# A reordered opening, and weights and the next rows held behind pair 0's gathers, in an attention, mixing and low-rank feed-forward kernel

## The reference

```python
# 1: attention over a block cache (window 128 + own tokens), 8 heads, 4 key heads of 32
q = rope(rms(x @ Wq.T) * (1 + qs), pos); k = rope(rms(x @ Wk.T) * (1 + ks), pos); v = x @ Wv.T
pos = lens[:, None] + arange(32)
k_blocks = k_blocks.at[table[b, pos // 16], :, pos % 16, :].set(k)   # and v_blocks with v
scores = q . k_all * SCALE, masked to pos - 128 < kpos <= pos
x = x + (softmax(scores) @ v_all) @ Wo.T
# 2, 3: a 32 x 32 matrix per sequence mixes its tokens; step 3 adds a bias
x = x + einsum(x, w1[cond]);  x = x + einsum(x, w2[subj]) + side[subj]
# 4: feed-forward, each linear with a low-rank part by the sequence's adapter
gate = x @ Wg + (x @ Ag[subj]) @ Bg[subj];  up = x @ Wu + (x @ Au[subj]) @ Bu[subj]
h = silu(gate) * up
x = x + h @ Wd + (h @ Ad[subj]) @ Bd[subj]
```

## Time and profile before

| | us |
|---|---|
| runs, median of 3 | 263.36 (260.64 to 263.76) |
| the profiled execution, own time | 262.86 |
| its span in the trace | 260.9 |
| PE busy, share of the span | 209.6, 80% |
| DVE busy | 140.6, 54% |
| ACT busy | 106.9, 41% |
| POOL busy | 82.8, 32% |
| mean granted clock of PE | 0.941 |

### The profile page before, as it was taken

The page is one execution under the profiler, slowest core; times in us unless marked ns, Lnnn a source line. Parts: engine busy times, 40 slices in busy tenths (PEclk is TensorE's granted clock), DMA queues, the critical chain, the costliest instruction groups (busy, mean ns, idle before and its releaser), DMA issues.

```text
span 260.9 us, 5090 instructions
## 1 busy us (share of the span) xinstructions
PE 209.6 (80%) x1993; PEld 190.3 (73%) x1993; DVE 140.6 (54%) x470; ACT 106.9 (41%) x290; POOL 82.8 (32%) x95
## 2 busy tenths in 40 slices
PE   2797969346858509994599979999988989989995
PEld 2785759245647408993598969988888989879995
DVE  1946877246675553396613763672375464135522
ACT  1615126587542551448102553381373345213310
POOL 3571037624467632007616036042421004000000
PEclk9979988968999956999689999999999999999999
DMA  6688979995863996753769202100400000010001
GB/s 192 153 178 142 168 185 237 433 189 86 133 186 97 256 170 81 105 82 92 149 122 178 71 3 71 32 0 23 123 0 3 0 1 3 3 40 3 0 0 43
DMA packets 64269, 26.28 MB, mean 101 GB/s; under 512 B 55941, under 2 KB 60933, under 8 KB 63653
## 3 DMA queue, kind: packets, MB, share of 16 engines
q1 hardware_dynamic: 60352, 15.07, 28.0%
q0 software_dynamic: 3104, 10.23, 16.3%
q10 hardware_dynamic: 788, 0.64, 0.8%
HBM read 18.87 MB, written 8.13 MB: 103 GB/s over the span
## 4 chain that ended last, share of the span: by engine, by line
PE 38%; issue 13%; DVE 12%; POOL 10%; SPq 10%; DMA 9%; ACT 7%; ACTq 0%; POOLq 0%; DVEq 0%
PE bank L1453 27%; SPq L612 5%; POOL far L685 4%; SPq L555 4%; ACT prob L806 3%; DVE prob L1097 3%; DMA near<-rows_of,place_i 3%; POOL prob L699 3%; DMA early<-in_kb,blk_i 3%; PE bank L1400 2%; PE bank L1439 2%; DMA k<-in_c 2%; DMA rows_of<-far_probs 2%; PE bank L1419 2%; DVE mask L1079 1%
## 5 line engine op out<-in xcount | busy, mean ns | idle before, releaser
L685 POOL DMA_INDIRECT far<-rows_of,place_i x32 | 32.3, 1008 | 63.3 <-issue 31.2
L806 ACT ACTIVATE prob<-prob,ntop,qscale 128x160 f32<-128x160 f32 x64 | 32.4, 508 | 15.7 <-DVE ntop L1103 15.7
L1453 PE MATMUL bank<-xf_high,gu_high 128*128 128x256 f32 x128 | 38.7, 303 | 0.0
L699 POOL TENSOR_TENSOR prob<-prob,rden 128x512 f32<-128x512 f32 x16 | 18.0, 1127 | 59.5 <-DVE rden L1109 59.5
L1453 PE MATMUL bank<-xf_high,gu_low 128*128 128x256 f32 x128 | 36.1, 282 | 0.0
L1453 PE MATMUL bank<-xf_low,gu_high 128*128 128x256 f32 x128 | 36.1, 282 | 0.0
L1133 DVE SCALAR_TENSOR_TENSOR gs<-th,bank 128x256 f32<-128x256 f32 x32 | 13.4, 420 | 28.5 <-ACT th L841 28.1
L1400 PE MATMUL bank<-k,prob 128*128 128x128 f32 x64 | 12.6, 329 | 17.9 <-POOL prob L699 17.9
L1453 PEld LDWEIGHTS bank<-xf_high,gu_high 128*128 128x128 f32 x128 | 24.4, 191 | 1.3 <-issue 0.9
L1453 PEld LDWEIGHTS bank<-xf_low,gu_high 128*128 128x128 f32 x128 | 24.4, 191 | 0.2
L841 ACT ACTIVATE th<-bank 128x256 f32<-128x256 f32 x32 | 12.0, 380 | 30.7 <-PE bank L1453 30.7
(11 more groups left out here) (218 smaller groups left out, 532.8 us busy)
## 6 DMA issues: line engine op xcount, KB each, us to landing
rows_of<-early SPq DMA_DIRECT2D x32, 144.0 KB
rows_of<-far_probs SPq DMA_DIRECT2D x2, 512.0 KB, 3.8
gu_raw<-in_Wg SPq DMA_DIRECT2D x2, 512.0 KB, 6.0
gu_raw<-in_Wu SPq DMA_DIRECT2D x2, 512.0 KB, 7.2
d_raw<-in_Wd SPq DMA_DIRECT2D x2, 512.0 KB, 5.6
out<-xs SPq DMA_DIRECT2D x8, 128.0 KB, 1.8
xs<-in_x ACTq DMA_DIRECT2D x1, 512.0 KB, 4.5
xs<-in_x SPq DMA_DIRECT2D x1, 512.0 KB, 5.8
```

The lines of the kernel that those rows point to most:

```text
L685: pool.indirect_dma_start(far[r][:, s, :], None, rows_of[t % 2], bass.IndirectOffsetOnAxis(ap=far_i[:, GB * n + s:GB * n + s + 1], axis=0) ...
L699: pool.tensor_tensor(v, v, over(scale, 2, P), ALU.mult).then_inc(prob_ready, 1)
L806: last = act.activation(v, v, ACT.Exp, bias=ntop[r][:, j:j + 1], scale=qscale[:, n, j:j + 1], accum_out=den[r][:, j:j + 1])
L1453: last = pe.matmul(dst, w[a], x[b], start=start and n == 0, stop=stop and n == 2)
```

## The change

The constants `k96` move from the third DMA of ACT's queue to the second of SP's. Two one-column activations load ACT's tables for Sin and Exp early. ACT copies the turned x ahead of the sine. On PE the small matmuls (scale, written blocks, later writes) move behind projections, and `project_q(1)` ahead of the slot matmuls. On DVE `k_finish(0)` moves ahead of `k_products(2)` and of the block diagonal, and `k_finish(1)` ahead of `same` and `mix_eye`. SP issues the new rows ahead of the mixing matrices, the adapter weights and g0 ahead of the matrices' way back, and then waits until the gathers of both groups of pair 0 have landed, with b0, u0, b1, the row copy, `scatter_rows(1)`, g1 and u1 behind that wait. In the lists ("first", 0) moves behind ("scores", 1); the low half of b1 and the mask of group 2 move into `FIRST_ORDER` behind the adapter product; the splits of g1 and u1 move behind the probabilities' transposes and behind pv.

```diff
--- before.py
+++ after.py
@@ -140,15 +140,16 @@
 
 
 START_ORDER = (
-    [("mask", 0), ("kt", 0), ("scores", 0), ("mask", 1), ("kt", 1), ("den", 0), ("first", 0), ("high", "a"), ("high", "g0"),
-     ("scores", 1), ("pt0", 0), ("prod", 0), ("pt1", 0), ("den", 1), ("gather", 0), ("gather", 1), ("load", 2),
+    [("mask", 0), ("kt", 0), ("scores", 0), ("mask", 1), ("kt", 1), ("den", 0), ("high", "a"), ("high", "g0"),
+     ("scores", 1), ("first", 0), ("pt0", 0), ("prod", 0), ("pt1", 0), ("den", 1), ("gather", 0), ("gather", 1), ("load", 2),
      ("low", "a"), ("low", "g0"), ("pv", 0), ("pt0", 1), ("wo", 0), ("high", "b0"), ("pt1", 1), ("mix", 0), ("pv", 1),
      ("xt", 0), ("xf", 0), ("low", "b0"), ("wo", 1), ("high", "u0"), ("low", "u0"), ("mix", 1), ("xt", 1), ("xf", 1),
-     ("high", "b1"), ("low", "b1"), ("mask", 2)])
+     ("high", "b1")])
 FIRST_ORDER = (
-    [("use", "a"), "lora", "adapt", ("use", "g0"), "gate0", ("first", 1), ("use", "u0"), ("use", "b1"), "up0",
-     ("kt", 0), ("prod", 1), ("scores", 0), ("mask", 1), ("split", "g1"), "gate1", "up1", ("den", 0), ("split", "u1"), "gate2",
-     ("pt0", 0), ("pt1", 0), "up2", "gate3", ("pv", 0), "up3", ("wo", 0), ("use", "g1"), "gate4", ("mix", 0),
+    [("use", "a"), "lora", "adapt", ("low", "b1"), ("mask", 0), ("use", "g0"), "gate0", ("first", 1), ("use", "u0"), ("use", "b1"),
+     "up0",
+     ("kt", 0), ("prod", 1), ("scores", 0), ("mask", 1), "gate1", "up1", ("den", 0), "gate2",
+     ("pt0", 0), ("pt1", 0), ("split", "g1"), "up2", "gate3", ("pv", 0), ("split", "u1"), "up3", ("wo", 0), ("use", "g1"), "gate4", ("mix", 0),
      ("gather", 0), ("load", 3), ("use", "u1"), "up4", ("split", "d0"), "gate5", "up5", ("kt", 1), ("split", "d1"),
      "gate6", "up6", ("scores", 1), ("mask", 2), "gate7", ("den", 1), ("split", "ad"), "up7", ("xt", 0), ("xf", 0),
      ("use", "d0"), ("use", "d1"), "down00", "down01", ("split", "bd"), ("pt0", 1), "down10", ("pt1", 1), "down11",
@@ -200,6 +201,7 @@
         k96 = sb("k96", [NW, C96_N])
         k32 = sb("k32", [B, C32_N])
         ones = sb("ones", [P, P])
+        primer = sb("primer", [P, 1])
 
         def c1(name):
             return k128[:, C128[name][0]:C128[name][1]]
@@ -535,6 +537,7 @@
         @block.sync
         def _(sp):
             sp.dma_start(len_i[:, 0:1], lens.rearrange("(b o) -> b o", o=1)).then_inc(lens_in, 16)
+            sp.dma_start(k96[:, :], c96).then_inc(k96_in, 16)
             sp.dma_start(k128[:, 0:C128["hide"][0]], c128[:, 0:C128["hide"][0]]).then_inc(k128_in, 16)
             sp.dma_start(wk_raw[:, :], Wk).then_inc(wvk_in, 16)
             sp.dma_start(wv_raw[:, :], Wv).then_inc(wvk_in, 16)
@@ -579,19 +582,21 @@
                              ).then_inc(w_in[name], 16)
 
             scatter_rows(0)
+            new_rows(0)
+            new_rows(1)
             sp.wait_ge(mix_eye, 1)
             for n in range(2):
                 sp.dma_start(mix_rows[n, :, :], mix_raw[:, n, :]).then_inc(mix_out, 16)
-            new_rows(0)
-            new_rows(1)
-            sp.wait_ge(zero_set, 2)
-            mix_blocks()
             for a, src in enumerate((Ag, Au)):
                 for k in range(KD):
                     at = (a * KD + k) * NR
                     sp.dma_start(a_raw[:, at:at + NR].rearrange("p (n r) -> p n r", r=RANK),
                                  src[:, k * P:(k + 1) * P, :].rearrange("n p r -> p n r")).then_inc(w_in["a"], 16)
             gate_up("g0", Wg, 0, lower)
+            sp.wait_ge(zero_set, 2)
+            mix_blocks()
+            for r in R:
+                sp.wait_ge(kv_in[r], 16 * (GB + 1))
             for a, src in enumerate((Bg, Bu)):
                 sp.dma_start(b_raw[:, a * FF:(a + 1) * FF], src.rearrange("n r f -> (n r) f")).then_inc(w_in[f"b{a}"], 16)
                 if a == 0:
@@ -726,7 +731,6 @@
         def _(act):
             act.dma_start(k32[:, :], c32).then_inc(k32_in, 16)
             act.dma_start(xs[:, 0:4, :], x[0:16, :, :].rearrange("(g s) t d -> (s t) g d", s=GB)).then_inc(x_in[0], 16)
-            act.dma_start(k96[:, :], c96).then_inc(k96_in, 16)
             for n, s in enumerate((ks, qs)):
                 act.dma_start(scale_in_row[:, n, :], s.rearrange("(o d) -> o d", o=1)).then_inc(scale_in, 16)
             act.dma_start(subj_i[:, :], subj.rearrange("(b o) -> b o", o=1)).then_inc(subj_in, 16)
@@ -737,14 +741,17 @@
                 act.copy(x_t[:, k, 4 * half:4 * half + 4, :].rearrange("p g t -> p (g t)"),
                          bank[1 + 2 * half + k][:, :]).then_inc(xt_ready, 1)
 
+            act.wait_ge(ones_set, 1)
+            act.activation(primer[:, :], ones[:, 0:1], ACT.Sin)
             act.wait_ge(w_psum, 1)
             act.copy(w_vkq[:, :, 0:KV], bank[5][:, :].rearrange("p (k c) -> p k c", k=KD)).then_inc(w_ready, 1)
+            for half in range(2):
+                for k in range(KD):
+                    take_xt(half, k)
             act.wait_ge(arg_ready, 1)
             act.activation(trig[:, :, :, :].rearrange("p a g f -> p (a g f)"),
                            rest[:, :, :, :].rearrange("p a g f -> p (a g f)"), ACT.Sin).then_inc(sin_ready, 1)
-            for half in range(2):
-                for k in range(KD):
-                    take_xt(half, k)
+
             def take_vk(i):
 
                 act.wait_ge(vk_psum, i + 1)
@@ -790,6 +797,7 @@
             act.copy(bias[:, :], small("bias")).then_inc(bias_ready, 1)
             take_qt(0)
             root(3, NG * G, NG * (G + H))
+            act.activation(primer[:, :], ones[:, 0:1], ACT.Exp)
             for i in range(1, NPAIR):
                 take_qt(i)
 
@@ -949,10 +957,6 @@
             dve.wait_ge(sin_ready, 1)
             dve.tensor_scalar(adapt[:, :], small("subj"), c1("adapter"), None, ALU.is_equal)
             rope_table(0)
-            dve.wait_ge(wrow_psum, 1)
-            dve.scalar_tensor_tensor(later_same[:, :], wblk_rows, wblk_f[:, 0:1], c9("later"), ALU.is_equal, ALU.mult
-                                     ).then_inc(later_ready, 1)
-
             def products(dst_s, dst_c, src, n, groups, nh):
 
                 for a in range(2):
@@ -997,27 +1001,30 @@
                                   over(rstd[:, lo:hi].rearrange("p (t h) -> p t h", h=G), 3, HD), ALU.mult
                                   ).then_inc(k_ready, 1)
 
+            k_products(0)
             rope_table(1)
-            for i in range(2):
-                k_products(i)
+            k_products(1)
+            dve.wait_ge(wrow_psum, 1)
+            dve.scalar_tensor_tensor(later_same[:, :], wblk_rows, wblk_f[:, 0:1], c9("later"), ALU.is_equal, ALU.mult
+                                     ).then_inc(later_ready, 1)
             dve.wait_ge(later_psum, 1)
             dve.scalar_tensor_tensor(alive[:, :], later_writes, 0.0, written[:, :], ALU.is_equal, ALU.mult
                                      ).then_inc(alive_ready, 1)
+            k_finish(0)
+            k_products(2)
             for t in range(NT):
                 dve.wait_ge(blk_in[t], 16)
             then(dve.tensor_copy(blk_f[:, :], blk_i[:, :]))
             dve.tensor_tensor(blk_diag[:, :, :], over(ident[0:BP, 0:BP], 1, NT), over(blk_f[:, :], 2, BP), ALU.mult
                               ).then_inc(bdiag_ready, 1)
-            k_finish(0)
-            for i in range(2, 4):
-                k_products(i)
+            k_products(3)
+            k_finish(1)
             dve.wait_ge(brow_psum, 1)
             dve.tensor_scalar(same[:, :, :, :].rearrange("w j t b -> w t j b"),
                               blk_rows.rearrange("w (t j b) -> w t j b", t=NT, j=SLOTS), wblk_f[:, 0:1], None,
                               ALU.is_equal).then_inc(same_ready, 1)
             dve.wait_ge(mix_in, 32)
             dve.tensor_scalar(mix_raw[:, :, ::T + 1], mix_raw[:, :, ::T + 1], 1.0, None, ALU.add).then_inc(mix_eye, 1)
-            k_finish(1)
 
             dve.wait_ge(rows_psum, 1)
             won, own = small("rows", B), c3("own")
@@ -1229,11 +1236,6 @@
                         last = pe.transpose(bank[1 + 2 * half + k][:, g * P:(g + 1) * P],
                                             xs[:, 4 * half + g, k * P:(k + 1) * P], ident)
                     last.then_inc(xt_psum, 1)
-            pe.wait_ge(scale_ready, 1)
-            pe.matmul(small("scale"), ones[0:1, :], scale_row[:, :, :, :].rearrange("p a n d -> p (a n d)"),
-                      start=True, stop=True)
-            pe.matmul(small("subj"), ones[0:B, :], diag_subj[:, :], start=True, stop=True).then_inc(scale_psum, 1)
-
             def project(i, dst, cols, done):
 
                 for t in range(2):
@@ -1265,14 +1267,19 @@
                                              stop=(k == 1))
                 last.then_inc(qt_psum, 1)
 
+            pe.wait_ge(w_ready, 1)
+            project_vk(0)
+            pe.wait_ge(scale_ready, 1)
+            pe.matmul(small("scale"), ones[0:1, :], scale_row[:, :, :, :].rearrange("p a n d -> p (a n d)"),
```

(11 more changed lines are left out.)

## The result

| | before | after |
|---|---|---|
| median time, us | 263.56 (260.64 to 266.45, 4 runs) | 268.08 (266.59 to 270.58, 4 runs) |
| profiled execution: own time; span, us | 262.86; 260.9 | 268.21; 266.4 |
| ratio of the times | | 1.0221, 95% interval 1.0164 to 1.0278 |
| ratio in a second comparison, on the chip of e9 to e12 (e12, below) | | 1.0144, interval 1.0067 to 1.022 |

A forecast was written before the change was run, and what follows sets the result against it. Two serial paths bound the kernel: compute, and blocks, scatter, gather. Later place table 0.8 + K 0.7 - 0.45 spare at group 2's gather = +1.05 us on 262.86 or 263.36: 264.2 us, range 260.2 to 267.6.

The forecast's parts named there:

- The opening's order: Start of kernel: first projection 1.7 us sooner, diagonal behind the square root at 24.7, place table at 36.2 instead of 34.13.
- The gain of the earlier k96: Start of kernel: k96 lands up to 2 us sooner or no sooner, first scatter with it; costed at nothing.
- The clock of the query projections: PE before the place table: four projections in 7.4 us; slow clock allowed only at the first early projection, upper bound 37.4.
- Pair 0: First pair's attention: group 1's gather lands in 2.5 us, at 50.8 instead of 55.51; 0.9 of 4.7 us reach the compute path.
- The load of Exp's table: ScalarE before pair 0's exponentials: early load removes 1.28 us that lay inside a wait for row maxima; counted 0.
- K's landing: Pair 1's K block gather: issued 0.8 us later, crowded by released transfers, 0.7 us longer than 11.5 (bounds 0 and 4.4).
- The second scatter: SP's scatter of pair 1's blocks: starts 1.5 us later, and so does the near gather behind it; 9.17 us before.
- PE waits, and the shift is carried to the end: PE starts pair 1's keys at 84.3, 1.05 us late; all through group 3's normalisation 1.05 later, nothing changed behind 126.
- The normalisation of group 2: On POOL: earlier and without a split beside it, 1 to 2 us, but the gain ends in the wait before 125.76.
- Rival 2: Released transfers crowd the K load and a slow first projection adds 1.2: 266.7 in the middle, 269.1 at most; chance 0.20.
- Rival 1 and 3: Block path not later, compute gain passes through, 261.3, chance 0.22; and compute gains plus less crowded adapter stretch, 257.5, 0.05.
- Rival 4: The hold on SP's queue does nothing that counts: 263.4, inside the first forecast, whose chance of 0.50 includes it.

The follow-up runs named there:

- e9: Changed kernel with the row copy issued ahead of the hold and b0, u0, b1 issued by ScalarE's queue: 264.81 us, ratio 1.0069.
- e12: The changed kernel itself measured again, on another chip: 266.86 us, ratio 1.0144.
- e7: Changed kernel, hold kept, with query projections 0 and 1 ahead of the block rows on PE, the third ahead of the slot matmuls: 264.4 us, ratio 1.0045.
- e10: Changed kernel without the hold and with query projections ahead of the block rows on PE: 261.76 us, ratio 0.9931.
- e11: Changed kernel without the hold, query projections ahead of the block rows, b0, u0, b1 issued behind the second scatter: 259.89 us, ratio 0.9895.
- e1: Changed kernel without the hold (the two waits for pair 0's gathers taken out): 264.9 us, ratio 1.0109.
- e2: Kernel before with only the hold added, ahead of b0, u0, b1: 264.3 us, ratio 1.0038.
- e4: Changed kernel, hold kept, with the block diagonal put back ahead of k_finish(0) on DVE: 264.63 us, ratio 1.0112.
- e3: Kernel before with only the change's new step lists: 263.05 us, ratio 1.0022.
- e8: Changed kernel without the hold, with query projections ahead of the block rows and block diagonal ahead of k_finish(0): 263.51 us, the kernel before's median on its chip.
- e6: Changed kernel with b0, u0, b1 issued by ScalarE's queue, the row copy still on SP behind the hold: 266.78 us, ratio 1.0116.
- e5: Changed kernel with the row copy issued ahead of the hold, b0, u0, b1 still behind it on SP: 265.93 us, ratio 1.0064.

## Why the prediction was wrong, point by point

**The opening's order: right.** The first projection started at 11.34 (11.1 predicted), the four ended at 19.63 (20.3). The diagonal started at 23.93 (24.7) and the first query projection at 27.19 (27.3). The new rows did not decide. The first gather was released by the place table. The gain of the earlier k96 was nothing, as costed: the first gather of block numbers was issued 2.2 us sooner but took 6.1 us to land, and POOL issued pair 0's K at 11.05 where it had done so at 11.32.

**The clock of the query projections: a term that failed by its size, 2.0 us.** The step gave four projections 1.99 + 5.45 = 7.4 us, the numbers of a PE that had hardly waited. I had given half a clock a place only at the first early projection, where it did not occur, and did not ask for it behind the new wait of 4.87 us, where it did. Two of the four took 5.97 in place of 3.9. The place table came at 38.22, past even the upper bound of 37.4. e7, e10 and e11 have the projections ahead of the wait and ran at full clock. This term is not small in the time. The prediction let 0.8 us of the late table reach pair 1's blocks, but e1, the change with nothing held, is 1.1% above the kernel before, about 2.9 us, and e10, with another order on PE alone, is 1.8% below e1. How much of that is the clock and how much the wait itself no run separates.

**Pair 0: right in its mechanism.** The gather of group 1 landed in 3.6 us instead of 8.0 (2.5 predicted), and the next scores started at 58.15 where 56.8 was predicted. The place table alone was 2.0 later than predicted, so what follows it came out 0.6 better than the step said. The exponentials of group 1 began 3.5 us after the end of group 0's. The load of Exp's table was hidden before, as costed.

**K's landing: wrong in sign.** Predicted 12.2 us (11.5 + 0.7), measured 7.74. I took the released transfers to crowd K, since they follow it by 2.4 us. In all eight profiles with weights released behind K (after, e12, e2, e4 to e7, e9) it took 7.1 to 8.0 us, and 7.1 with nothing released beside it (e11). Transfers released long ahead of K are those that can cost it: 11.5 before, and 9.1, 9.9, 8.1 and 10.7 in e1, e3, e8 and e10. The packets of the changed kernel show why, first at 54 to 57 us, where there are none of SP's queue, then SP's at 57 to 62:

```profile
q0 software_dynamic: 86, 0.61, 95.5%
```

```profile
q1 hardware_dynamic: 160, 0.48, 45.3%
```

The weights were issued from 54.09 on, but moved nothing until 57 and only 0.48 MB by 62. At 62 to 66 the engines moved 2.14 MB, when K had landed and V was landing. In this stretch each transfer moved mostly behind those issued ahead of it: the weights behind the blocks, the scatter behind the weights. V shared more with them than K did: it took 9.7 to 11.4 us in the same eight profiles, and 8.1 in e11.

**The second scatter: the step that failed most.** The prediction moves its start by 1.5 us and carries its 9.17 us over unchanged. It took 16.36. No bound was put on this term, though the argument let four large transfers go at 50.8, 11 us ahead of its scatter; as measured they went 5.4 us ahead of it. They were costed against K's landing, which they did not hurt, and not against the next transfer on the path. In the two profiles +7.19 here is more than the whole shift; -3.80 by K's landing and -1.22 - 0.24 behind it gave part back. Each of the two failures alone left the time inside the range of 260.2 to 267.6 (264.4 in e7, 264.9 in e1). With both it was 268.08, just outside, and 266.86 in e12, inside.

**PE waits, and the shift is carried to the end: right, with another size.** PE waited for pair 1's gather (4.0 us, keys at 88.04, 84.3 predicted), group 3's normalisation was released by POOL's own gathers at 131.22 (126.8 predicted), and behind it nothing changed: 266.4 - 131.22 = 135.2, and 260.9 - 125.76 = 135.1. A term was missing: the clock behind PE's wait, +1.40 in the keys and the mixer product. It came with the longer waits only: the keys' four matmuls took 1.11 to 1.12 us behind waits of 2.5 to 4.0 us (after, e4, e6, e7, e12), and 0.66 behind waits of 1.0 to 1.3 (e2, e5, e9). The normalisation of group 2 took 1.03 and not 1.99 us, as said, and gained nothing.

**The rivals.** Rival 2 had the right sign and blamed the released transfers, but for crowding K, and its price hung on K landing later than 60.3; K landed sooner, and it was the scatter that they delayed. Its 266.7 came near the time for a reason it did not name. Rival 1 and 3 did not come. Rival 4, that the hold does nothing, is refuted by e7 against e10, which differ by the hold alone: 1.0045 and 0.9931, two intervals that do not overlap (each against the kernel before on its own chip), so 1.1% of the time is the hold, about 3 us.

**What stays open.** Why a transfer's packets do not start while those issued ahead of it, even in another queue, still move: whether they come into the queue late or wait in it cannot be seen, and no run changed the block gathers' queue. e6's scatter was 1.4 us shorter than the changed kernel's with the same four transfers; its row copy landed 4.9 us behind the scatter's start and not 9.8, which may be the reason, but no run tests it. And e11 may owe part of its gain to the opening alone: e10 and e11 differ by 0.4% with intervals that overlap.

## What to carry to other kernels

A wait that holds transfers back moves their load; it does not remove it. Cost the released bytes against every transfer that is issued behind them within their landing time, most of all against one that is on the serial path (here 9.2 us became 16.4), and first try to put the urgent transfer ahead of the held ones. Where a reorder puts a new idle time in front of matmuls, price those matmuls at both clock levels.

## What the runs showed of the hardware that was not expected

- A scatter of 8 issues of 144 KB took 8.2 to 9.2 us alone, 13.77 beside three transfers of 512 KB and 16.0 to 16.4 beside those and the row copy. The queue that the three stood in made no difference (13.77 both times). The excess lies ahead of its first packets: they came 1.3 us behind the start of its issues in e11, but over 4 us in e9 and over 7 us in the changed kernel.
- K's block gather, issued by POOL, landed in 7.1 to 8.0 us with 1.5 MB of weights released 1.5 to 3.3 us behind it, and in 7.1 without. In the changed kernel those weights moved nothing for the first 3 us. V's gather, issued 1.3 us behind K's, did take longer: 9.7 to 11.4 us against 8.1.
- The length of PE's idle time alone does not order its clock. After 4.87 us idle it was 0.50, for over 5 us; after 2.11 in e3 and 2.74 in e4 it fell to 0.50 too; after 2.36 in e7 it stayed at 1.00. In e7 dense projections follow at once; in e3 and e4 small matmuls and a second gap of 0.74 us come first.
- The same four small gathers of block numbers had all landed by 21.6 us in e4 and by 22.5 in e8, issued within 0.2 us of the same time. That spread decides whether DVE's order holds PE.
